# A two-layer conditioned block on one core: first norm spread from its root, stacked condition parts, a new order of the steps

## Chip, core and metric

One of the eight cores of a Trainium2 chip runs the whole kernel. The time is the device time of one execution in microseconds, from the first to the last instruction with what lies around them. TensorE is PE in the profile, VectorE DVE, ScalarE ACT, GpSimd POOL, and SP is the sync engine, which here only issues DMAs.

## What is computed

128 sequences of 64 tokens with 256 features go through a transformer block whose norms are modulated by a condition per sequence, and then through a graph attention with 20 keys. Everything is float32. Cut to what matters:

```python
mods = silu(c) @ adaln_w + adaln_b              # per sequence: shift, scale, gate, twice
x_mod = rms(x) * (1 + scale_msa) + shift_msa    # first norm
q, k, v = split(x_mod @ qkv_w); q, k = rope(rms(q)), rope(rms(k))
x = x + gate_msa * (softmax(q k^T / 4) v @ proj_w + proj_b)
h = rms(x) * (1 + scale_mlp) + shift_mlp        # second norm
x = x + gate_mlp * (silu(h @ w1) * (h @ w3) @ w2)
# graph layer: v = x, q = c
row_zero = v.sum(-1) == 0
self_feat = [v, where(row_zero, 0, q)] @ W_self.T + b_self
for d in range(2):                              # adjacency and its transpose, 20 keys, 11 labels
    aff = where(A.sum(-1) > 0, q1 k1^T / 4, NEG) + A @ w_bias
    out += softmax(aff) @ kv @ Wout[d]
y = v + relu(self_feat + out)
```

## The kernel before

The 128 sequences are cut into 32 blocks of 4 sequences (MB), 256 tokens (MT). Activations lie transposed, features on the partitions in DC = 2 chunks of 128, tokens along the free axis. A float32 matmul of the large weights is made of three products of rounded parts: `w_lo` and `w_hi` with the high part, `w_hi` with the low part of the activation (`high_terms`, `low_terms`, all recorded at L456, the helper `linear`). ScalarE rounds the high part (L831, L878, L893, L905, L916), GpSimd subtracts it for the low part (L1290).

All work of a block is cut into named steps, and for each engine a list in `ORDER` (L79 to L114) says in which order it does them. An entry (a, step, n) does part n of the step for block m + a in iteration m, so several blocks are in flight: on TensorE in iteration m the graph layer of block m, the MLP of block m + 1, the attention of block m + 2 and the first norm's transposition of block m + 3. `run_steps` (L148) writes out the first and last iterations and makes a loop of the others. Engines meet only by semaphores: `wait` waits for this block's producer, `wait_free` for the last reader of a PSUM bank (`BANK`, L71 to L75, says which of the eight 2 KB banks a step writes).

First norm, before. SP loads x by tokens (x_in). ScalarE squares it with a running sum (L811), GpSimd makes the mean's inverse root (L1278, L1280), ScalarE multiplies the token rows by it (L818), TensorE transposes the rows in four pieces (L496), VectorE multiplies by the scale out of PSUM (L1057) and adds the shift (L1076). VectorE first copies the block's conditions to a small tile (L1051, and L1062 for the second norm), by a product with ones.

Second norm, before. ScalarE squares x1 (L824); TensorE sums over features with a column of 1/256, tile by tile and chunk by chunk, four matmuls that the profile shows as eight instructions (L504); VectorE adds epsilon (L1047), GpSimd takes the power -1/2 (L1286), TensorE transposes the broadcast root, which spreads it over all partitions (L511), and VectorE multiplies x1, already scaled by GpSimd (L1312), by it (L1067), then adds the shift.

Self feature, before. TensorE sums the rows (`rowsum`, a product with ones) and multiplies by W_self (L674 to L681). VectorE makes a gate of 128 rows (L1179): row b is one where the token belongs to sequence b and its sum isn't zero. `self_cond` (L683) then adds the condition part with four matmuls, `cond_lo` and `cond_hi` by two output chunks. VectorE adds the bias (L1188).

Other steps that the text names. VectorE: `edge_masks` (L1201 to L1204, its scaling L1202), `score_max` and `score` (L1120, L1125: maximum and subtraction of the attention's scores), `k1` (L1211), `score1_bias`, `score1_max`, `score1` (graph scores), `mix` (L1131, L1134), `mix1` (L1250), `qkv` (L1087 to L1100), `rope_scale` (L1104), `rope` (L1110), `mlp_up` (L1159 to L1168), `mlp_down` (L1173), `edges` (L1195), `out` (L1256). TensorE: `heads` (L540), `score` (L557), `probsT` (L577), `mix` (L592), `mixT` (L601), `v1` (L727), `score1` (L744), `probsT1` (L761), `mix1` (L775). GpSimd: `heads` spreads the keys (L1302), `proj` adds the residual (L1323), `mlp_down` adds x1 (L1327).

At the start SP loads the condition, nine small constants, the first weight pieces and x; ScalarE's queue loads the condition weights. VectorE waits for all constants (L978) before it forms the silu of the condition, TensorE makes the twelve modulations (L476), VectorE adds their biases (L1033). Weight pieces are staged in free tiles (`HOME`) and split by ScalarE and VectorE behind certain steps (`HIGH_PARTS`, `LOW_PARTS`).

## Time and profile before

| | us |
|---|---|
| median of 3 runs | 1485.19 (1482.28 to 1488.89) |
| profiled execution, its own time | 1483.07 |
| its span, first to last instruction | 1481.2 |
| TensorE busy in it | 1345.6 (91%) |
| VectorE busy | 1189.3 (80%) |
| ScalarE busy | 899.2 (61%) |
| GpSimd busy | 657.3 (44%) |

The mean granted TensorE clock is 0.975 of full speed. Times below are from one profiled execution, counted from the start of its span. Matmuls are pipelined and their ends are modelled: in a run of them the next starts before the end of the one before, so the length of a step on TensorE is best read from its start to the start of what follows.

### The profile page before, as it was taken

To read this page: it belongs to the slowest core of one execution; us is meant where nothing else is said; L and a number is where in the kernel's file an instruction comes from. 1 tells how busy PE (TensorE), PEld (TensorE's weight loads), DVE (VectorE), ACT (ScalarE), POOL (GpSimd) and SP (SyncE) were. 2 spreads that over 40 slices of the span, in tenths; PEclk is the share of its full clock that TensorE was granted. 3 is DMA by queue.
4 is the path that set the end of the run, shared out by engine and by line. 5 is a ranking of instruction groups with operands and counts; after the bars stand their busy time and mean duration, and the time that the engine had idled before them with its cause. 6 is when DMAs were issued, how large, how long until landed. Compare 5 with 4: busy or idle time off the path is not lost. (4 is left out here: it accounts for less than half of the span.)

```text
span 1481.2 us, 51674 instructions
## 1 busy us (share of the span) xinstructions
PE 1345.6 (91%) x20532; PEld 1243.1 (84%) x20532; DVE 1189.3 (80%) x2137; ACT 899.2 (61%) x1744; POOL 657.3 (44%) x580
## 2 busy tenths in 40 slices
PE   4589999999999999999999999999999999999985
PEld 3479888888888888988888898888888888888885
DVE  5558888888888888888888888888888888888853
ACT  3456566667666666666666676666667666666632
POOL 0134444544444454444445444444544444454441
PEclk9589999999999999999999999999999999999998
DMA  5200111110011111001111100111110011110000
GB/s 171 65 27 2 36 35 33 33 33 21 12 33 33 33 33 33 17 16 33 33 33 33 33 12 21 33 33 33 33 33 12 21 33 33 33 33 26 3 27 16
DMA packets 40307, 47.28 MB, mean 32 GB/s; under 512 B 3536, under 2 KB 38224, under 8 KB 40272
## 3 DMA queue, kind: packets, MB, share of 16 engines
q1 hardware_dynamic: 39424, 44.94, 10.0%
q10 hardware_dynamic: 848, 1.84, 0.3%
q8 instruction: 26, 0.43, 0.1%
q14 instruction: 9, 0.07, 0.0%
HBM read 38.38 MB, written 8.39 MB: 32 GB/s over the span
## 5 line engine op out<-in xcount | busy, mean ns | idle before, releaser
L456 PE MATMUL psum<-nh,w_lo 128*128 128x256 f32 x704 | 181.8, 293 | 0.7 <-DVE gf L1168 0.6
L1290 POOL TENSOR_TENSOR nl<-xn,nh 128x512 fp32r<-128x512 f32 x64 | 82.8, 1294 | 221.3 <-ACT nh L831 221.3
L456 PE MATMUL psum<-nh,w_hi 128*128 128x256 f32 x704 | 172.7, 280 | 0.9 <-issue 0.9
L1290 POOL TENSOR_TENSOR gl<-gf,gh 128x512 fp32r<-128x512 f32 x96 | 123.6, 1287 | 105.2 <-ACT gh L893 105.2
L456 PEld LDWEIGHTS psum<-nh,w_lo 128*128 128x128 f32 x704 | 133.6, 190 | 7.5 <-issue 7.0
L456 PEld LDWEIGHTS psum<-nh,w_hi 128*128 128x128 f32 x704 | 133.8, 190 | 1.1 <-issue 1.1
L1346 POOL TENSOR_TENSOR e<-e,inv 128x640 f32<-128x640 f32 x64 | 81.5, 1273 | 99.4 <-DVE inv L1245 99.3
L456 PE MATMUL psum<-nl,w_hi 128*128 128x256 f32 x704 | 115.6, 283 | 0.0
L831 ACT ACTIVATE nh<-xn 128x512 fp32r<-128x512 f32 x64 | 40.4, 631 | 106.3 <-DVE xn L1076 106.1
L1302 POOL TENSOR_TENSOR kbd<-qkT,hmask 128x512 f32<-128x512 f32 x64 | 66.5, 1040 | 86.2 <-ACT qkT L859 86.2
L456 PEld LDWEIGHTS psum<-nl,w_hi 128*128 128x128 f32 x704 | 95.3, 189 | 3.4
L864 ACT ACTIVATE e<-e 128x1024 f32<-128x1024 f32 x64 | 68.1, 1064 | 49.6 <-DVE e L1125 49.6
L1087 DVE TENSOR_TENSOR qs<-psum,sinw 128x512 f32<-128x512 f32 x64 | 44.2, 691 | 66.5 <-ACT qk_sq L839 62.2
L1327 POOL TENSOR_TENSOR x<-x 128x512 f32<-128x512 f32 x32 | 41.0, 1282 | 124.1 <-DVE x L1173 124.1
L456 PE MATMUL psum<-qkv_lo,nh 128*128 128x512 f32 (+1 forms) x256 | 86.2, 348 | 4.8 <-ACT nh L831 4.8
L456 PE MATMUL psum<-gh,w_lo 128*128 128x256 f32 x320 | 83.0, 291 | 0.0
L456 PE MATMUL psum<-qkv_hi,nh 128*128 128x512 f32 (+1 forms) x256 | 82.2, 343 | 0.0
L1120 DVE TENSOR_REDUCE mx<-psum 128x16 f32<-128x1024 f32 x64 | 78.1, 1220 | 4.1 <-PE psum L557 0.8
L893 ACT ACTIVATE gh<-gf 128x512 fp32r<-128x512 f32 x96 | 60.7, 632 | 32.4 <-DVE gf L1168 30.3
L456 PE MATMUL psum<-gh,w_hi 128*128 128x256 f32 x320 | 79.5, 280 | 0.0
L592 PE MATMUL psum<-vb,pT 128*64 128x34 f32 x2048 | 73.7, 227 | 6.3 <-ACT pT L873 3.2
L1125 DVE TENSOR_TENSOR e<-psum,mx 128x1024 f32<-128x1024 f32 x64 | 76.5, 1195 | 3.4
(187 smaller groups left out, 4418.2 us busy)
## 6 DMA issues: line engine op xcount, KB each, us to landing
adj<-in_adj SPq DMA_DIRECT2D x32, 440.0 KB, 3.3
x_in<-in_x SPq DMA_DIRECT2D x32, 256.0 KB, 3.0
x_res<-in_xT SPq DMA_DIRECT2D x32, 256.0 KB, 3.2
out_T<-y SPq DMA_DIRECT2D x32, 256.0 KB, 2.2
e<-in_adaln ACTq DMA_DIRECT2D x2, 512.0 KB, 5.5
stage<-in_qkv SPq DMA_DIRECT2D x2, 384.0 KB, 5.6
pT<-in_w SPq DMA_DIRECT2D x2, 384.0 KB, 7.2
stage<-in_w SPq DMA_DIRECT2D x2, 384.0 KB, 6.6
```

Source lines behind the costliest of these rows:

```text
L456: last = nc.tensor.matmul(out, lhsT, rhs, start=start and i == 0, stop=stop and i == len(terms) - 1)
L592: last = nc.tensor.matmul(mix_ps[t][s * S:(s + 1) * S, j, :], pT0[:, j, s * S:(s + 1) * S], vb[:, t, s, j, :], start=True, stop=True, tile ...
L831: nc.scalar.activation(nh[norm][:, :, :], xn[norm][:, :, :], ACT.Copy).then_inc(normed_hi[norm].sem, 1)
L864: nc.scalar.activation(e0[t][:, :, :], e0[t][:, :, :], ACT.Exp, scale=DH ** -0.5).then_inc(exps.sem, 1)
L893: nc.scalar.activation(gh[:, 2 * n:2 * n + 2, :], gf[:, :, :], ACT.Copy).then_inc(g_hi.sem, 1)
L1087: nc.vector.tensor_tensor(qs[:, :, :, :], qk_ps, sinw[:, :, :].unsqueeze(2).to_broadcast([P, 2, H, DH]), ALU.mult).then_inc(sin_part.sem, 1)
L1120: nc.vector.tensor_reduce(mx0_v, s_v[t], AX.X, ALU.max).then_inc(maxima.sem, 1)
L1125: nc.vector.tensor_tensor(e0_v[t], s_v[t], mx0_v.unsqueeze(3).to_broadcast([P, NG, 4, S]), ALU.subtract).then_inc(shifted_s.sem, 1)
L1290: return nc.gpsimd.tensor_tensor(out, full, hi.bitcast(F32), ALU.subtract)
L1302: nc.gpsimd.tensor_tensor(kbd[:, t, :, :, :, :].rearrange("p c s h k -> p (c s) h k"), qkT[t][:, 1, :, :].rearrange("p c (s k) -> p (c s) ...
L1327: nc.gpsimd.tensor_tensor(x2[:, :, :], x2[:, :, :], x1[:, :, :], ALU.add).then_inc(x2_done.sem, 1)
L1346: nc.gpsimd.tensor_tensor(e_v, e_v, inv1[t][:, :].unsqueeze(2).to_broadcast([P, ND * H, NKV]), ALU.mult)\
```

## The change

- **First norm.** SP now also loads the transposed x into `xn[0]` (`load_xT`). GpSimd multiplies it by the scale (`norm0_scale`), TensorE transposes the broadcast root in two pieces (`norm0_apply`), VectorE multiplies by the spread root and adds the shift. The scaling of the token rows on ScalarE and the four transpositions are gone. ScalarE squares in place.
- **Squares summed by chunks.** A VectorE step `norm1_squares` adds the two chunks of the second norm's squares; TensorE sums two tiles in place of four pieces.
- **Stacked condition parts.** High and low part of the condition product are written to DRAM once; SP loads for each block 8 rows (high and low of four sequences). The gate has 8 rows, and `self_cond` has two matmuls in place of four.
- **Self bias** is added by ScalarE in place of VectorE. The copies of the block's conditions are gone: the steps read `mods` itself.
- **At first** VectorE waits for the constants after the condition's silu, ScalarE adds the biases of eight of the twelve modulations, and pieces of the weights are loaded in another order to other homes.
- **All orders and PSUM banks** are new.

The diff, cut to its core (bank waits, declarations and unchanged context left out):

```diff
 BANK = {
-    "xT": 4, "qk": (1, 5), "v": (2, 4), "heads": (0, 2), "probsT": (2, 6, 5, 3), "probsT1": (0, 2, 3, 7),
-    "mix": (6, 3), "q1": (1, 4), "score": 3, "score1": 3, "mixT": 6, "proj": 7, "norm1": 2, "up": (1, 2, 7),
-    "gate": (3, 7, 0), "down": 1, "rowsum": 5, "self": 0, "k1": 6, "v1": 0, "mix1": 2,
+    "xT": 6, "qk": (2, 3), "v": (7, 1), "heads": (7, 5), "probsT": (5, 4, 4, 0), "probsT1": (0, 5, 4, 7),
+    "mix": (5, 6), "q1": (4, 6), "score": 0, "score1": 0, "mixT": 6, "proj": 2, "norm1": 7, "up": (6, 4, 6),
+    "gate": (3, 1, 0), "down": 1, "rowsum": 3, "self": 4, "k1": 5, "v1": 7, "mix1": 5,
 }
 ORDER = {
     "PE": [
...
+        (2, "heads", 1), (1, "proj", 0), (0, "self", 0), (0, "self_cond", 0), (2, "score", 0), (0, "k1", 0),
+        (0, "q1", 0), (1, "norm1_mean", 0), (0, "q1", 1), (1, "norm1_apply", 0), (2, "probsT", 0),
+        (3, "norm0_apply", 0), (0, "score1", 0), (0, "v1", 0), (2, "mix", 0), (2, "probsT", 1), (1, "mlp_up", 0),
+        (1, "mlp_up", 1), (3, "qkv", 0), (0, "probsT1", 0), (2, "mix", 1), (3, "qkv", 1), (0, "mix1", 0),
+        (0, "probsT1", 1), (1, "mlp_up", 2), (0, "mix1", 1), (1, "mlp_down", 0), (1, "mlp_down", 1), (2, "mixT", 0),
+        (3, "heads", 0),
     ],
     "DVE": [
...
+        (2, "rope", 0), (2, "rope", 1), (0, "mlp_down", 0), (1, "mixT", 0), (1, "proj", 0), (0, "row_mask", 0),
+        (0, "edge_masks", 0), (2, "score_max", 0), (2, "score", 0), (1, "norm1_squares", 0), (2, "score_max", 1),
+        (1, "norm1_mean", 0), (0, "k1", 0), (2, "score", 1), (1, "norm1_apply", 0), (1, "norm1_shift", 0),
+        (3, "norm0_apply", 0), (3, "norm0_shift", 0), (0, "score1_bias", 0), (0, "score1_max", 0),
+        (0, "score1_bias", 1), (0, "score1", 0), (2, "mix", 0), (0, "score1_max", 1), (0, "soft1", 0),
+        (0, "soft1_inverse", 0), (1, "mlp_up", 0), (0, "score1", 1), (0, "soft1", 1), (0, "soft1_inverse", 1),
+        (1, "mlp_up", 1), (2, "mix", 1), (3, "qkv", 0), (3, "qkv", 1), (1, "mlp_up", 2), (0, "mix1", 0),
+        (1, "edges", 0), (3, "rope_scale", 0), (0, "out", 0),
     ],
     "Activation": [
...
+        (2, "rope_scale", 0), (0, "mlp_split", 2), (1, "mixT", 0), (2, "heads", 0), (2, "heads", 1),
+        (0, "x2_split", 0), (0, "self", 0), (1, "norm1_mean", 0), (0, "keys", 0), (0, "self_split", 0),
+        (3, "norm0_mean", 0), (2, "score", 0), (0, "q1", 0), (0, "q1", 1), (2, "probsT", 0), (2, "score", 1),
...
     "Pool": [
...
+        (1, "proj", 0), (0, "self_split", 0), (3, "norm0_mean", 0), (1, "norm1_mean", 0), (1, "norm1_scale", 0),
+        (3, "norm0_scale", 0), (1, "norm1_apply", 0), (3, "norm0_apply", 0), (0, "soft1", 0), (1, "mlp_up", 0),
+        (0, "soft1", 1), (1, "edges", 0), (1, "mlp_up", 1), (1, "mlp_up", 2), (1, "mlp_down", 0), (3, "heads", 0),
+        (1, "x2_split", 0), (3, "heads", 1),
     ],
     "SP": [
-        (3, "norm0_mean", 0), (2, "mlp_up", 0), (0, "out", 0), (2, "norm0_apply", 0),
+        (0, "self", 0), (3, "norm0_mean", 0), (1, "mlp_up", 0), (3, "norm0_scale", 0), (2, "norm0_apply", 0),
+        (0, "out", 0),
     ],
...
+            def load_xT(m, n):
+                wait_last(sp, normed_lo[0], m)
+                sp.dma_start(xn[0][:, :, :], x_v[:, :, bass.ds(m * MT, MT)]).then_inc(xT_in_s.sem, 16)
...
+            def load_cond_rows(m, n):
...
+                wait_last(sp, self_ps, m)
+                sp.dma_start(cond_rows[:, :].bitcast(F32), cond_parts[bass.ds(m, 1), :, :, :].rearrange("m i b n -> (m i b) n"))\
+                    .then_inc(cond_rows_s.sem, 16)
...
             def norm0_apply(m, n):
...
                 for t in range(TILES):
-                    for c in range(DC):
-                        last = nc.tensor.transpose(xT_ps[:, c, t * P:(t + 1) * P], x_tok[:, t, c * P:(c + 1) * P], ident[:, :])
-                last.then_inc(xT_done.sem, 1)
+                    last = nc.tensor.transpose(spread0_ps[:, t * P:(t + 1) * P],
+                                               rms_inv[0][:, t:t + 1].to_broadcast([P, P]), ident[:, :])
+                last.then_inc(spread[0].sem, 1)
...
                 for t in range(TILES):
-                    for c in range(DC):
-                        last = nc.tensor.matmul(ms1_ps[:, t:t + 1], x1_sq[:, c, t * P:(t + 1) * P],
-                                                mean_col[:, :], start=c == 0, stop=c == DC - 1)
+                    last = nc.tensor.matmul(ms1_ps[:, t:t + 1], x1_sq[:, 0, t * P:(t + 1) * P], mean_col[:, :],
+                                            start=True, stop=True)
...
             def self_cond(m, n):
                 wait(pe, row_gate, m, 1)
+                wait(pe, cond_rows_s, m, 16)
                 for o in both:
-                    last = linear(self_out[:, o, :], [(w[:, out_chunks[o]], gate[:, :]) for w in (cond_lo, cond_hi)], False, o == DC - 1)
+                    last = linear(self_out[:, o, :], [(cond_rows[:, out_chunks[o]], gate[:, :])], False, o == DC - 1)
...
+            def self_feat(m, n):                    # on ScalarE
+                wait(act, self_ps, m, 1)
+                wait_last(act, relu_done, m)
+                for o in range(DC):
+                    nc.scalar.activation(sf[:, o, :], self_out[:, o, :], ACT.Identity, bias=self_b[:, o:o + 1])\
+                        .then_inc(self_done.sem, 1)
...
+            def norm1_squares(m, n):
+                wait(dve, squares[1], m, 1)
+                nc.vector.tensor_tensor(x1_sq[:, 0, :], x1_sq[:, 0, :], x1_sq[:, 1, :], ALU.add).then_inc(square_sums.sem, 1)
...
-            def self_feat(m, n):
-                wait(dve, self_ps, m, 1)
-                wait_last(dve, relu_done, m)
-                for o in range(DC):
-                    nc.vector.tensor_scalar(sf[:, o, :], self_out[:, o, :], self_b[:, o:o + 1], None, ALU.add)\
-                        .then_inc(self_done.sem, 1)
...
+            def norm0_scale(m, n):                  # on GpSimd
+                wait(pool, xT_in_s, m, 16)
+                nc.gpsimd.tensor_tensor(by_seq(xn[0][:, :, :]), by_seq(xn[0][:, :, :]),
+                                        per_seq(mods[:, SCALE_A:SCALE_A + DC, bass.ds(m * MB, MB)]), ALU.mult)\
+                    .then_inc(scaled[0].sem, 1)
```

## Rows read from the trace of the kernel before

**Rows 1.** Busy time of the engines in one steady interval
```profile
core 0: us, PE busy (x) PEld busy (x) DVE busy (x) ACT busy (x) POOL busy (x), PEclk, DMA share, GB/s
700.00:743.30 43.30, 40.99 (x642) 37.97 (x642) 36.49 (x65) 27.73 (x55) 20.56 (x19) 1.00 0.10 29
```

**Rows 2.** Second root's transposition: ns min/median/max, first and last start us
```profile
L511 PE MATMUL psum<-ident,rms_inv x64: 270/272/474, 83.4 to 1423.8; 128*128 128x128 f32 x64
```

**Rows 3.** Timeline, TensorE, steady interval: start us, us, engine, line, operation
```profile
710.83 1.09 PE L577 MATMUL psum<-ident,e 128*128 128x128 f32 x8
...
712.75 1.13 PE L592 MATMUL psum<-vb,pT 128*64 128x34 f32 x32
...
716.96 0.39 PE L456 MATMUL psum<-aoh,proj_lo 128*128 128x256 f32 x1 [0.69 <-ACT aoh L878]
...
718.49 0.60 PE L496 MATMUL psum<-ident,x_tok 128*128 128x128 f32 x4
...
721.76 0.38 PE L456 MATMUL psum<-gate,cond_lo 128*128 128x256 f32 x1 [0.81 <-DVE gate L1179]
...
722.34 0.42 PE L456 MATMUL psum<-qkv_lo,nh 128*128 128x512 f32 x1
...
724.46 0.40 PE L456 MATMUL psum<-qkv_lo,nh 128*128 128x512 f32 x1
...
728.30 0.99 PE L504 MATMUL psum<-mean_col,x_sq 128*128 128x1 f32 x8
...
733.07 0.66 PE L540 MATMUL psum<-ident,qr 128*128 128x128 f32 x4 [0.71 <-DVE qr L1110]
733.66 1.51 PE L744 MATMUL psum<-kbd,q1T 32*64 32x40 f32 x128
...
735.52 0.36 PE L456 MATMUL psum<-nh,w_lo 128*128 128x256 f32 x1
...
743.55 1.21 PE L557 MATMUL psum<-kbd,qkT 32*64 32x128 f32 x64
```

**Rows 4.** Masks' scaling on VectorE: ns min/median/max, first and last start us
```profile
L1202 DVE TENSOR_SCALAR edge_n<-edge_n x32: 194/1193/1207, 104.0 to 1442.1; 128x80 f32<-128x80 f32 x32
```

**Rows 5.** Timeline, VectorE, the same interval
```profile
702.21 1.22 DVE L1120 TENSOR_REDUCE mx<-psum 128x16 f32<-128x1024 f32 x1
...
707.33 0.41 DVE L1162 SCALAR_TENSOR_TENSOR gf<-th,psum 128x256 f32<-128x256 f32 x1
...
708.30 0.69 DVE L1168 TENSOR_TENSOR gf<-gf,psum 128x512 f32<-128x512 f32 x1
709.62 1.07 DVE L1201 TENSOR_REDUCE edge_v<-q1T 128x80 f32<-128x880 f32 x1 [0.63 <-POOL q1T L1331]
710.60 1.19 DVE L1202 TENSOR_SCALAR edge_n<-edge_n 128x80 f32<-128x80 f32 x1
...
712.05 0.25 DVE L1131 RECIPROCAL inv<-psum 128x16 f32<-128x16 f32 x1
...
712.74 0.88 DVE L1250 SCALAR_TENSOR_TENSOR sf<-psum,bout,sf 128x256 f32<-128x256 f32 x2
...
725.28 0.69 DVE L1087 TENSOR_TENSOR qs<-psum,sinw 128x512 f32<-128x512 f32 x1 [1.87 <-ACT qk_sq L839]
...
730.51 1.25 DVE L1211 SCALAR_TENSOR_TENSOR kbd<-psum,colb,hmask 128x160 f32<-128x160 f32 x4
731.67 0.54 DVE L1104 RECIPROCAL qk_inv<-qk_root 128x64 f32<-128x64 f32 x1
```

**Rows 6.** Timeline, GpSimd, the same interval
```profile
710.46 1.28 POOL L1290 TENSOR_TENSOR gl<-gf,gh 128x512 fp32r<-128x512 f32 x1 [0.88 <-ACT gh L893]
...
736.53 1.03 POOL L1302 TENSOR_TENSOR kbd<-qkT,hmask 128x512 f32<-128x512 f32 x1
```

**Rows 7.** DMA issues: KB each, median us from issue to landing
```profile
x_res<-in_xT SPq DMA_DIRECT2D x32, 256.0 KB, 3.2
...
edge_b<-in_edge_b SPq DMA_DIRECT2D x1, 0.5 KB, 5.5
```

**Rows 8.** Waits: us in total, times, longest
```profile
DVE th L981 <- DMA freq<-in_freq: 5.0, 1, 5.0
```

More of the change, by code:

```diff
@@ L80 @@
     "PE": [
-        (0, "self", 0), (0, "self_cond", 0), (2, "qkv", 0), (2, "qkv", 1), (0, "k1", 0), (1, "norm1_mean", 0),
-        (0, "q1", 0), (0, "q1", 1), (1, "norm1_apply", 0), (2, "heads", 0), (0, "score1", 0), (2, "heads", 1),
-        (1, "mlp_up", 0), (0, "v1", 0), (1, "mlp_up", 1), (2, "score", 0), (0, "probsT1", 0), (1, "mlp_up", 2),
-        (1, "mlp_down", 0), (2, "probsT", 0), (0, "probsT1", 1), (0, "mix1", 0), (2, "mix", 0), (2, "probsT", 1),
-        (0, "mix1", 1), (2, "mix", 1), (1, "mlp_down", 1), (2, "mixT", 0), (2, "proj", 0), (3, "norm0_apply", 0),
+        (2, "heads", 1), (1, "proj", 0), (0, "self", 0), (0, "self_cond", 0), (2, "score", 0), (0, "k1", 0),
@@ L86 @@
+        (0, "q1", 0), (1, "norm1_mean", 0), (0, "q1", 1), (1, "norm1_apply", 0), (2, "probsT", 0),
[3 more added lines that the diff above has]
+        (3, "heads", 0),
     ],
     "DVE": [
-        (1, "mlp_up", 2), (1, "edge_masks", 0), (2, "mix", 0), (0, "mix1", 0), (0, "out", 0), (2, "mix", 1),
@@ L89 @@
-        (1, "mlp_down", 0), (2, "mixT", 0), (2, "edges", 0), (2, "proj", 0), (3, "norm0_scale", 0),
-        (3, "norm0_shift", 0), (1, "row_mask", 0), (1, "self", 0), (3, "qkv", 0), (3, "qkv", 1), (2, "norm1_mean", 0),
[3 rows of a table removed]
-        (2, "mlp_up", 1), (1, "soft1", 1), (3, "score_max", 0), (3, "score", 0), (3, "score_max", 1),
-        (1, "soft1_inverse", 1), (3, "score", 1),
+        (2, "rope", 0), (2, "rope", 1), (0, "mlp_down", 0), (1, "mixT", 0), (1, "proj", 0), (0, "row_mask", 0),
+        (0, "edge_masks", 0), (2, "score_max", 0), (2, "score", 0), (1, "norm1_squares", 0), (2, "score_max", 1),
[4 rows of a table added]
@@ L96 @@
+        (1, "mlp_up", 1), (2, "mix", 1), (3, "qkv", 0), (3, "qkv", 1), (1, "mlp_up", 2), (0, "mix1", 0),
+        (1, "edges", 0), (3, "rope_scale", 0), (0, "out", 0),
     ],
     "Activation": [
-        (2, "qkv", 1), (2, "rope_scale", 0), (0, "q1", 0), (0, "q1", 1), (2, "heads", 0), (1, "norm1_apply", 0),
-        (1, "edges", 0), (1, "mlp_up", 0), (2, "heads", 1), (0, "score1", 0), (1, "mlp_split", 0), (1, "mlp_up", 1),
-        (0, "v1", 0), (0, "score1", 1), (1, "mlp_split", 1), (0, "probsT1", 0), (2, "score", 0), (3, "norm0_mean", 0),
@@ L101 @@
-        (1, "mlp_up", 2), (2, "probsT", 0), (2, "score", 1), (1, "mlp_split", 2), (0, "probsT1", 1), (2, "probsT", 1),
-        (3, "norm0_rows", 0), (2, "mixT", 0), (1, "x2_split", 0), (3, "norm0_apply", 0), (1, "self_split", 0),
-        (3, "qkv", 0), (1, "keys", 0), (2, "norm1_mean", 0),
+        (2, "rope_scale", 0), (0, "mlp_split", 2), (1, "mixT", 0), (2, "heads", 0), (2, "heads", 1),
+        (0, "x2_split", 0), (0, "self", 0), (1, "norm1_mean", 0), (0, "keys", 0), (0, "self_split", 0),
@@ L104 @@
+        (3, "norm0_mean", 0), (2, "score", 0), (0, "q1", 0), (0, "q1", 1), (2, "probsT", 0), (2, "score", 1),
+        (1, "norm1_apply", 0), (0, "v1", 0), (3, "norm0_apply", 0), (1, "edges", 0), (0, "score1", 0),
+        (2, "probsT", 1), (1, "mlp_up", 0), (1, "mlp_split", 0), (0, "score1", 1), (1, "mlp_up", 1),
+        (0, "probsT1", 0), (3, "qkv", 0), (1, "mlp_split", 1), (3, "qkv", 1), (0, "probsT1", 1), (1, "mlp_up", 2),
     ],
     "Pool": [
-        (0, "x2_split", 0), (2, "norm0_apply", 0), (1, "proj", 0), (0, "self_split", 0), (1, "norm1_scale", 0),
@@ L210, in build_program @@
         rms_inv = [sb(f"rms_inv{i}", [P, TILES]) for i in range(2)]
-        mod = [sb(f"mod{i}", [P, NMOD, MB]) for i in range(2)]
         nh = [sb(f"nh{i}", [P, DC, MT], F32R) for i in range(2)]
@@ L248, in build_program @@
         sf = sb("sf", [P, DC, MT])
-        gate = sb("gate", [P, MT], F32R)
+        gate = sb("gate", [2 * MB, MT], F32R)
+        cond_rows = sb("cond_rows", [2 * MB, D], F32R)
         kv = sb("kv", [P, DC, MB, NKP])
@@ L678, in self_feat @@
                 wait(pe, x2_lo, m, 1)
-                linear(rowsum_ps, [(ones_r[:, :], nl[1][:, c, :]) for c in both], start=False).then_inc(rowsum.sem, 1)
+                linear(rowsum_ps, [(ones_r[:, 0:M_SUM], nl[1][:, c, :]) for c in both], start=False).then_inc(rowsum.sem, 1)
                 for o in both:
@@ L1144, in proj @@
             def proj(m, n):
+                if isinstance(m, int) and m == 0:
+                    dve.wait_ge(mods_set_a.sem, NMOD - 4)
                 wait(dve, proj_done, m, 1)
```

284 lines of the change are left out of this document (146 added, 138 removed), and 3 rows, old and new, of the table ORDER.

## The prediction

> **What bounds the kernel now.** I read the busy table by stage first. In one steady stretch of 43.3 us TensorE is busy 41.0, VectorE 36.5, ScalarE 27.7, GpSimd 20.6, and the granted clock is full [rows 1]. One block of four sequences takes that long: the transposition of the second norm's root runs from 83.4 to 1423.8 over 32 blocks, 31 intervals of 43.24 us [rows 2]. So three parts make the span: 83.4 us of filling, 31 intervals, and 57.4 us (1481.2 less 1423.8) of draining. Then the timeline of TensorE in one interval. It stands still only three times: 0.69 us before the projection (ScalarE's rounding of the mixed heads), 0.81 before the condition step (VectorE's row gate), 0.71 before the first heads transposition (VectorE's rotated heads) [rows 3]. So in the steady part TensorE is the bound, with 2.2 us of waits, and an edit pays if it takes TensorE's work or one of these waits away, until VectorE, 6.8 us behind, is reached.
>
> **What the parts do to each engine, per block.**
> *TensorE.* The condition step goes from four matmuls to two; the four take 0.58 us (721.76 to 722.34) [rows 3], so 0.3 goes. A matmul with 8 rows in place of 128 has no row of its own; I take it as long as a full one, and even at nothing it would give only 0.3 more. The four transpositions of normed rows (0.60, of which 0.27, the length of a single one [rows 2], is the tail of the last) become two of a root: 0.2 less. The means go from eight instructions (0.99 with tail) to four: 0.4 less [rows 3]. The projection's wait of 0.69 goes, since both heads transpositions now stand between mixT and proj (0.6 each); the gate's wait shrinks from 0.8 to about 0.2, since VectorE's first-norm steps no longer stand ahead of the gate. TensorE alone, with the heads' wait gone too, could do 43.3 - 0.3 - 0.2 - 0.4 - 0.7 - 0.6 - 0.7 = 40.4 us.
> *VectorE.* Two copies of the conditions go (48 elements, 0.2 each, as the quickest of the masks' scalings of 80 [rows 4]) and the self bias (two of 0.44, as mix1's two of the same size) goes to ScalarE; the sum of squares by chunks comes, 256 elements, which costs about 0.4 as half the 0.69 of 512 [rows 5]. The first norm's multiplication stays. Net 0.9 less: 35.6 busy. *ScalarE* loses two scalings of x and gains two biases of the same width: nothing, and it idles a third of the time [rows 1]. Its table loads stay two a block. *GpSimd* gains the first norm's scale, 1.05 us as its other products of this form (kbd 1.03) [rows 6], laid between two waits; if its cover went, the MLP's low part would come 1.05 later, and TensorE has mix and a transposition before it. *DMA.* A second transposed x (256 KB) and an 8 KB condition load a block, 0.1 of the DMA time now being used [rows 1]; the x load lands in some 3.2 us [rows 7] and is issued, behind the edge masks' wait, some 6 us before its use. SP's queue is in order: the condition load (waits for the self feature of the block before, long done), x, edges (wait for the masks, at 7.8 on the clock below), transposed x, residual x (waits for GpSimd's addition, at 6.8), the store (waits for out, the last step). Behind the masks' wait only loads stand that have over 5 us to their use, so I cost the queue at nothing but for the condition rows, a rival below.
>
> **The new order, followed round once.** The sum of work doesn't say what the order gives, so I place the steps on a clock that starts when VectorE begins mlp_down(0), its third step.
> 1. VectorE 0.69 for its 512 elements; GpSimd in its new order adds (1.28, as all its products of 512 plain elements), spreads keys (1.03, now between) and takes the low part of x2 (1.28): with four handoffs of 0.05 it is 4.5 us [rows 5, 6].
> 2. TensorE's last row sums, the gate (256 elements, 0.41 as the MLP's row of that size), handoffs: 0.9. At 5.4.
> 3. VectorE: edge masks 2.43 (709.62 to 712.05); both maxima and both subtractions 4.87 (702.21 to 707.33 less a reciprocal's 0.25); sum of squares 0.4; k1 1.25: 9.0 us with the small ones [rows 5]. At 14.4.
> 4. TensorE could be at score1(0) at about 13.9, but that shares a PSUM bank with score(2) and waits for VectorE's second subtraction. Then score1 1.45, mix and transposition 1.06 and 1.02, both MLP stages with v1 8.03 (735.52 to 743.55), qkv 2.12 (722.34 to 724.46), transposition 1.02, mix 1.06: 15.7, each row less the 0.07 by which it overlaps the next, with handoffs 15.8 [rows 3]. At 30.2.
> 5. VectorE: mix 0.69, two qkv steps 5.16 (725.28 to 730.51, less 0.07), third MLP stage 1.66, mix1 0.88, edges 1.07 (the reduction of 880 elements), rope_scale 0.65 (0.54 and a handoff), out and two ropes of 0.69, less the 0.08 by which operations in a row overlap: 11.9 us [rows 5]. At 42.1, where mlp_down of the next block begins. Its matmuls were done 0.8 us before.
> So the interval is **42.1 us**, VectorE's chain and no more TensorE alone: 1.7 us above TensorE's bound, 1.2 below 43.3. One term has two values in the trace: the masks' scaling of 80 elements takes 1193 ns as a rule but 194 at its quickest [rows 4]; in the steady interval it starts 0.14 us after a GpSimd operation and ends as that ends [rows 5, 6]. In the new order GpSimd's addition of the residual lies there for only some 0.4, so 0.6 could be won back; I keep it as reserve for steps that now meet GpSimd and didn't before.
>
> **A rule beside it.** In the trace the pair just named shows VectorE held for about 1.0 us, while VectorE's additions of two SBUF operands fall where GpSimd idles [rows 4, 6]. The Trainium skill (SBUF — State Buffer, Who interferes with whom) says that also a VectorE instruction with two SBUF inputs and a GpSimd one that reads SBUF exclude each other for a whole instruction. The trace agrees for the scaling alone. What that could do is the second rival.
>
> **Filling and draining.** VectorE waits 5.0 us at the start for the last small constant before it makes the conditions [rows 8]; the new code waits after. At best all 5.0 is won. Against it, qkv(1) now stands ahead of proj(0): two of 2.12, twice that at half clock, up to 8.5 us. Between -5 and +8.5 I take +1: the first root at 84. Block 0 to 1 lacks the graph steps, the last interval the qkv steps (5.2 of VectorE): 37 us each. The last block's chain is the same: 57.4.
> Sum: 84 + 37 + 29 x 42.1 + 37 + 57.4 = 1436.3 us span; the profiled execution had 1.9 outside its span (1483.1 against 1481.2), so 1438 against its 1483. The median of the runs, 1485.2, is 2.1 higher: **1440 against the median**.
>
> **Rivals.**
> *TensorE stays the bound (0.12).* VectorE's steps overlap their neighbours a little more than I summed, the masks' 0.6 comes free, and score1's wait disappears: 40.4 us. Speaks for it: VectorE would be busy 35.6 of 40.4. Against: the waits before self, the means, the root and score1 would all have to go at once. 29 x 1.7 less: 1391.
> *GpSimd holds VectorE (0.16).* In my round norm0_shift starts within 0.1 us of GpSimd's low part, the squares' sum meets its roots, the additions of qkv meet gl. Each held step in a chain piece costs about 1.0 (1193 less 194) [rows 4]. One such step: 43.1, 1440 + 29 = 1469 (0.08). From the second on, 2.0 against the 1.2 gained, the change loses: **1498 with two, 1527 with three (0.08 together)**. Against it: norm0_shift has 1.4 us of slack before TensorE's second mix, and no two-operand addition of the trace was ever held. By the rule of the Trainium skill's SBUF page all three could be held.
> *The condition rows come late (0.07).* SP issues their load after the store, 0.5 us before my clock's zero, and the condition step wants them at 5.4. A load lands in 3.2 us as a rule, the smallest took 5.5 at the start [rows 7]: on time both ways. At 7.2 us each block would lose 1.3: 1440 + 38 = 1478. So this is the case in which the new form brings nothing.
> *The fill is mis-sized*: -6 to +8 on any case.
>
> **Chances.** My own round 0.65 (1420 to 1460, the interval 41.5 to 42.7). About 0.5%, 7.4 us, is what a measurement of this kernel can tell from no change, so faster means below 1478: 0.65 + 0.12 + 0.08 and nothing of the late rows, 0.85. Slower 0.08, the two or more held steps; same 0.07. The range leaves out most of the first rival and the losing case: 1400 to 1472.
>
> **What would show it.** Interval between the second norm's transpositions near 42.1; no wait of TensorE before proj, about 0.2 before the condition step, 0.5 before score1 on VectorE's subtraction and 0.5 before self on ScalarE's rounding; VectorE at 85%. Wrong would be: an interval at 40.4 with VectorE waiting before mlp_down; a two-operand VectorE step of 1.5 us; TensorE waiting for a DMA before the condition step; a first root far from 84.

## The result, and the profile after

The changed kernel takes 1421.39 us in the median of four runs (1416.22 to 1426.24), the kernel before 1485.87 on the same chip: a ratio of 0.9566, with a 95% interval of 0.9521 to 0.9612. The profiled execution has a span of 1416.1 us and a mean granted clock of 0.977. Its page's busy times:
```profile
PE 1342.2 (95%) x20276; PEld 1229.1 (87%) x20276; DVE 1135.2 (80%) x2033; ACT 878.6 (62%) x1752; POOL 712.1 (50%) x612
```

The changed kernel's transposition of the second norm's root, one pair a block (first and last start; against [rows 2]):
```profile
L541 PE MATMUL psum<-ident,rms_inv x64: 272/272/476, 79.1 to 1358.3; 128*128 128x128 f32 x64
```
and its busy time in one steady interval (against [rows 1]; columns: PE, PEld, DVE, ACT, POOL, granted clock, DMA share, GB/s):
```profile
700.00:741.40 41.40, 41.13 (x635) 37.68 (x634) 34.78 (x63) 26.97 (x55) 22.33 (x19) 1.00 0.12 36
```
Filling takes 79.1 us instead of 83.4, draining 57.8 (1416.1 less 1358.3) instead of 57.4, and the 31 intervals sum to 1279.2 instead of 1340.4. So 61 of the 65 us came from the intervals. In the steady part each is 41.41 us (43.29 before). "Interval" below is always the median distance of these transpositions in the trace.

TensorE now shows busy for 99% of an interval, and its recorded waits over 28 intervals are gone. Waits of TensorE in the changed kernel, 160 to 1340 us (us in total, times, longest):
```profile
PE psum L775 <- issue: 1.0, 2, 0.7
```
The timeline of VectorE in one steady interval (start, us, engine, line, operation; idle before it and what ended that), cut to the rows used, against [rows 5]:
```profile
718.43 0.26 DVE L1162 RECIPROCAL inv<-psum 128x16 f32<-128x16 f32 x1 [1.36 <-PE psum L622]
...
720.85 1.36 DVE L1130 TENSOR_TENSOR qr<-qc,qs 128x256 f32<-128x256 f32 x2
...
724.04 0.75 DVE L1130 TENSOR_TENSOR qr<-qc,qs 128x256 f32<-128x256 f32 x2
...
727.06 1.06 DVE L1221 TENSOR_REDUCE edge_n<-adj 128x80 f32<-128x880 int32 x1
...
729.04 1.28 DVE L1141 TENSOR_TENSOR qr<-qr,qk_inv 128x512 f32<-128x512 f32 x2
730.24 0.68 DVE L1206 TENSOR_TENSOR x<-psum,mods 128x512 f32<-128x512 f32 x1
731.33 0.69 DVE L1171 TENSOR_TENSOR aol<-psum,aoh 128x512 fp32r<-128x512 f32 x1 [0.40 <-ACT aoh L911]
733.28 0.88 DVE L1182 SCALAR_TENSOR_TENSOR x<-psum,colb,mods 128x256 f32<-128x256 f32 x2 [1.26 <-PE psum L486]
735.13 0.41 DVE L1212 SCALAR_TENSOR_TENSOR gate<-psum,hot 8x256 fp32r<-8x256 f32 x1 [0.97 <-PE psum L486]
735.47 1.05 DVE L1227 TENSOR_REDUCE edge_v<-q1T 128x80 f32<-128x880 f32 x1
736.44 0.38 DVE L1228 TENSOR_SCALAR edge_n<-edge_n 128x80 f32<-128x80 f32 x1
```
Two things are to be seen. From the second mix (718.43) to mlp_down (730.24) VectorE has no idle time at all, and before and after that it waits for TensorE (1.36, 1.26, 0.97). This is the round of the prediction in its outline: TensorE's stretch, then VectorE's, then short steps by turns. Who closes the stretch between the condition step and score1 is another question; it is answered below. And the first pair of L1130 takes 1.36 us, the second 0.75: the first runs beside a GpSimd instruction. GpSimd in the same interval, against [rows 6]:
```profile
720.30 1.29 POOL L1315 TENSOR_TENSOR gl<-gf,gh 128x512 fp32r<-128x512 f32 x1 [1.36 <-ACT gh L926]
727.26 1.29 POOL L1315 TENSOR_TENSOR gl<-gf,gh 128x512 fp32r<-128x512 f32 x1 [5.67 <-ACT gh L926]
731.00 1.29 POOL L1360 TENSOR_TENSOR x<-x 128x512 f32<-128x512 f32 x1 [2.45 <-DVE x L1206]
```
On my clock (mlp_down at 730.24 is 0) the condition step's matmuls stand at 5.44:
```profile
735.68 0.49 PE L486 MATMUL psum<-gate,cond_rows 8*128 8x256 f32 x2
```
VectorE's second subtraction of the attention's scores, and TensorE's score1 behind it:
```profile
742.65 1.21 DVE L1156 TENSOR_TENSOR e<-psum,mx 128x1024 f32<-128x1024 f32 x1
```
```profile
744.26 1.50 PE L775 MATMUL psum<-kbd,q1T 32*64 32x40 f32 x128
```
The subtraction is done at 743.86, and score1 starts 0.40 later; the prediction had score1 wait for it. Over the steady blocks the two stand at 13.6 and 14.0 on the clock (medians).

### The profile page after: what moved, and what is told of

Its sections match the earlier page's. It is cut to its first block, busy times and chain, and to the rows that moved or that the text cites. A ratio compares the mean times of both kernels' runs of the same rounds, so it can differ in the third digit from the quotient of the medians.

```text
span 1416.1 us, 51305 instructions
## 1 busy us (share of the span) xinstructions
PE 1342.2 (95%) x20276; PEld 1229.1 (87%) x20276; DVE 1135.2 (80%) x2033; ACT 878.6 (62%) x1752; POOL 712.1 (50%) x612
## 4 chain that ended last, share of the span: by engine, by line
PE 73%; issue 9%; POOL 7%; ACT 3%; DVE 1%; ACTq 0%; POOLq 0%; DVEq 0%
PE psum L486 39%; PE psum L607 5%; PE psum L622 5%; PE psum L728 4%; PE psum L792 4%; PE psum L758 4%; PE psum L775 3%; POOL nl L1315 3%; PE psum L587 3%; PE psum L806 2%; POOL gl L1315 2%; POOL kbd L1327 2%; ACT gh L926 1%; PE psum L534 1%; ACT qkT L892 1%
## 5 line engine op out<-in xcount | busy, mean ns | idle before, releaser
L486 PE MATMUL psum<-nh,w_hi 128*128 128x256 f32 x704 | 176.8, 282 | 0.0
L1315 POOL TENSOR_TENSOR nl<-xn,nh 128x512 fp32r<-128x512 f32 x64 | 99.2, 1551 | 127.3 <-ACT nh L864 127.3
L946 ACT ACTIVATE sf<-psum,colb 128x256 f32<-128x256 f32 x64 | 26.8, 470 | 103.3 <-PE psum L486 103.3
L1151 DVE TENSOR_REDUCE mx<-psum 128x16 f32<-128x1024 f32 x64 | 78.1, 1221 | 14.4 <-PE psum L587 14.1
L911 ACT ACTIVATE aoh<-psum 128x512 fp32r<-128x512 f32 x32 | 19.1, 598 | 109.2 <-PE psum L631 109.2
L607 PE MATMUL psum<-ident,e 128*128 128x128 f32 x512 | 77.9, 289 | 4.3 <-ACT e L897 4.2
L622 PEld LDWEIGHTS psum<-vb,pT 128*64 128x64 f32 x2048 | 66.6, 140 | 12.8 <-issue 12.5
```

What stands on the lines that cost most here:

```text
L486: last = nc.tensor.matmul(out, lhsT, rhs, start=start and i == 0, stop=stop and i == len(terms) - 1)
L607: last = nc.tensor.transpose(pT_out[t][j // 4][:, j % 4, :], e0[t][:, 2 * pair(j):2 * pair(j) + 2, :].rearrange("p h s -> p (h s)"), ident ...
L622: last = nc.tensor.matmul(mix_ps[t][s * S:(s + 1) * S, j, :], pT0[:, j, s * S:(s + 1) * S], vb[:, t, s, j, :], start=True, stop=True, tile ...
L1151: nc.vector.tensor_reduce(mx0_v, s_v[t], AX.X, ALU.max).then_inc(maxima.sem, 1)
L1315: return nc.gpsimd.tensor_tensor(out, full, hi.bitcast(F32), ALU.subtract)
```

## The experiments

The theory was that the interval is a round through both engines: TensorE from score1 to the second mix (piece 4), VectorE from there to mlp_down (piece 5), and a chain of short steps between mlp_down and score1 (pieces 1 to 3). The rival was that TensorE's work alone is the bound, as 99% busy suggests. All ratios are against the kernel before on the same chip.

**Six matmuls fewer, at two places.** These two runs tell the theories apart. Both leave out six of the MLP's matmuls, those with the low part of the weight (so that part of x·w is not computed), one run in the second stage, one in the third:
```
-  linear(out[:, c, :], high_terms(w, out_chunks[j], nh[1], both), c == 0, False)
+  terms = high_terms(w, out_chunks[j], nh[1], both)
+  linear(out[:, c, :], terms[1::2] if n == 1 and (name, c) != ("w3", 1) else terms, c == 0, False)
   (the other run: if n == 2)
```


> In the second MLP stage six of its 24 matmuls are left out (the low part of the weight for three of four output chunks), some 0.75 us of TensorE's time, in the stretch between score1 and the second mix where VectorE waits for TensorE. Both theories (TensorE's work alone is the bound; TensorE and VectorE take turns in one round) expect the interval 0.7 shorter, 40.7, and some 1400 us.

> In the third MLP stage six of its 18 matmuls are left out, the same 0.75 us of TensorE's time, but beside the stretch in which my round runs through VectorE (second mix to mlp_down). TensorE's work alone as the bound: interval 40.7 and 1400 us, as in the run above. The round by turns: VectorE begins mlp_down 0.3 us after TensorE's last matmul for it, so the interval stays at 41.3 to 41.4, 1417 to 1421 us.

Measured: in piece 4 1403.04 us (1401.88 to 1407.19), ratio 0.9467 (0.944 to 0.9495), interval 40.67, 0.74 shorter. In piece 5 1424.63 us (1420.51 to 1426.06), 0.9596 (0.9569 to 0.9624), interval 41.42, no shorter. The same work is worth its full time at one place and nothing at the other. The second root's transposition, the run in piece 4 and then the run in piece 5:
```profile
L541 PE MATMUL psum<-ident,rms_inv x64: 272/272/473, 78.2 to 1338.5; 128*128 128x128 f32 x64
```
```profile
L541 PE MATMUL psum<-ident,rms_inv x64: 270/272/473, 79.2 to 1363.9; 128*128 128x128 f32 x64
```
Of the run in piece 5 also TensorE's waits and the busy windows, 160 to 1340 us:
```profile
PE psum L486 <- POOL gl L1316: 8.1, 28, 0.3
```
```profile
160.00:1340.00 1180.00, 1158.33 (x17851) 1052.14 (x17850) 988.02 (x1762) 765.94 (x1530) 632.47 (x538) 1.00 0.11 36
```
In the run in piece 5, TensorE's third MLP stage is 0.67 us shorter, from its start to the start of what follows, but mlp_down behind it is 0.48 longer and the projection 0.16. Only 0.3 of that is recorded as a wait, for GpSimd's low part of the gated values, which itself waits for VectorE's and ScalarE's steps of the third stage; the rest stands in a busy time that contains standing still (it falls from 1170.64, shown below, to 1158.33, by 0.43 an interval). TensorE's work alone is not the bound, although it shows 99% busy. The rival fell.

**Self bias back on VectorE.** In the new order, right behind the row gate:
```
 DVE: (1, "proj", 0), (0, "row_mask", 0), + (0, "self", 0), (0, "edge_masks", 0), ...
 ACT: (0, "x2_split", 0), - (0, "self", 0), (1, "norm1_mean", 0), ...
```


> The changed kernel with the self bias back on VectorE, between the gate and the edge masks. Loop theory: VectorE waits for self there and takes 0.9, so score_max starts about 1.2 us later and TensorE's score1, which has only some 0.2 us to spare, waits; interval up by 0.8 to 1.1, span about 1445. Rival (VectorE has slack, TensorE's work is the bound): within 0.2 us of 41.4, span 1416 to 1422.

Measured: 1451.65 us, ratio 0.9802 (0.9775 to 0.983), interval 42.27, 0.86 longer. TensorE's matmuls didn't change at all. The cost is VectorE's, as the round says, but TensorE meets it before the means of the second norm and not before score1, where it was expected (160 to 1340 us):
```profile
PE psum L534 <- DVE x_sq L1085: 12.9, 28, 0.5
```
That 0.86 is near the two biases' own 0.88 is in part chance: the masks start 1.5 later, as VectorE also waits for the self feature's matmuls (0.66), and 0.6 of it is won back, since VectorE no longer waits for the scores (0.39) and the masks' scaling isn't held (0.19).

**The other three parts, undone one by one in the new order.** First norm by token rows (two scalings of x on ScalarE, four transpositions on TensorE):
```
- transpose(spread0_ps[:, t * P:(t + 1) * P], rms_inv[0][:, t:t + 1].to_broadcast([P, P]), ident)
+ for c in range(DC): transpose(xT_ps[:, c, t * P:(t + 1) * P], x_tok[:, t, c * P:(c + 1) * P], ident)
+ ACT norm0_rows: activation(x_tok[:, t, :], x_in[:, t, :], ACT.Identity, scale=rms_inv[0][:, t:t + 1])
```


> The changed kernel with the first norm by token rows as before: two scalings on ScalarE between its q1 steps, four transpositions in place of two, no scale on GpSimd, no second load of transposed x. TensorE's work theory: 0.1 to 0.2 more per block, span 1419 to 1422. Loop theory: ScalarE's 0.9 falls where it has 0.56 to spare, 0.3 later for the probabilities' copies, interval 41.4 to 41.7, span 1416 to 1425. If the spread root were the main gain of the change: over 1440.

Measured 1426.13, ratio 0.9613 (0.9586 to 0.9639), interval 41.57. Squares not summed by chunks:
```
- nc.tensor.matmul(ms1_ps[:, t:t + 1], x1_sq[:, 0, t * P:(t + 1) * P], mean_col[:, :], start=True, stop=True)
+ for c in range(DC): nc.tensor.matmul(ms1_ps[:, t:t + 1], x1_sq[:, c, ...], mean_col[:, :], start=c == 0, ...)
```


> The changed kernel (interval 41.40 us) with TensorE summing all four pieces of squares again and no sum by chunks on VectorE. TensorE's own work sets the interval: 0.4 more, 41.8, span about 1429. The round through VectorE sets it: VectorE's stretch from edge masks to the second subtraction is 0.37 shorter, nothing or a little less, 41.2 to 41.4, span 1410 to 1416.

Measured 1432.46, ratio 0.9656 (0.9624 to 0.9689), interval 41.66. This is a miss of the round as I had it: with VectorE closing the stretch up to score1, less work for VectorE should have cost nothing (41.2 to 41.4). TensorE's four more instructions set the time there; it is nearer to the other case's 41.8. Condition step as before, 128 rows, four matmuls, no load:
```
- linear(self_out[:, o, :], [(cond_rows[:, out_chunks[o]], gate[:, :])], ...)
+ linear(self_out[:, o, :], [(w[:, out_chunks[o]], gate[:, :]) for w in (cond_lo, cond_hi)], ...)
```


> The changed kernel with the 128-row gate, four condition matmuls and no load of condition rows. They stand in the round itself (gate, condition step, score) and in TensorE's work, so both theories say 0.2 more: 41.6, span about 1423. If the load of the rows were felt in the changed kernel, this would be no slower or faster, 41.4 or less.

Measured 1428.37, ratio 0.9641 (0.9606 to 0.9676), interval 41.60. The intervals grow by 0.16, 0.25 and 0.19. The copies of the block's conditions stay away in every run here, so what their removal is worth was not measured. The medians of the first and third lie within their runs' scatter of the changed kernel's, so the interval of the trace is the better witness there.

**All parts, old order.** Every new operation, with the order and the PSUM banks of before; the chunk sum stands between the two qkv steps on VectorE:
```
 DVE: (3, "norm0_shift", 0), (1, "row_mask", 0), (3, "qkv", 0), + (2, "norm1_squares", 0), (3, "qkv", 1), ...
 ACT: (1, "x2_split", 0), (3, "norm0_apply", 0), + (1, "self", 0), (1, "self_split", 0), ...
 SP:  (3, "norm0_mean", 0), + (3, "norm0_scale", 0), (2, "mlp_up", 0), + (1, "self", 0), (0, "out", 0), ...
```


> All the new operations (spread root, sum of squares by chunks, 8 condition rows, bias on ScalarE, new start) in the old order with the old banks. If the parts bring what their instructions cost on TensorE (0.3 + 0.1 + 0.5) and the waits before proj (0.7) and before the condition step (0.8) stay: interval 43.3 - 0.9 = 42.4, span about 1453. If the order were worth nothing: 41.4 and about 1416 to 1425. If the parts are worth nothing by themselves: 43.3 and about 1478.

Measured: 1482.1 (1480.25 to 1484.62), ratio 1.0005 (0.9992 to 1.0017), interval 43.47: nothing was gained. A miss of 1.1 us an interval. The waits of TensorE there, 160 to 1340 us:
```profile
PE psum L568 <- DVE qr L1139: 29.0, 27, 1.1
PE psum L484 <- ACT aoh L909: 18.5, 27, 0.7
PE psum L484 <- DVE gate L1210: 16.9, 27, 0.6
```
Before, the same three stood at 0.71, 0.69 and 0.81 [rows 3]. TensorE had some 0.9 less to do. The gate's wait fell by 0.2, the wait for the rotated heads, which VectorE finishes in one unbroken stretch from the first qkv step, grew by 0.4. The rest of the saving is lost in steps that show busy; the next run says more on where.

**The same without the chunk sum.** The sum is VectorE's in that stretch, so it was suspected:
```
-  (3, "qkv", 0), (2, "norm1_squares", 0), (3, "qkv", 1), ...    and the means over both chunks on TensorE
+  (3, "qkv", 0), (3, "qkv", 1), ...
```


> The parts in the old order, but the squares of the second norm not summed by chunks on VectorE. If that sum, placed between the two steps of qkv, was what held the rotated heads and ate the parts' gain, TensorE's wait before the first heads transposition falls from 1.1 to 0.7, the interval from 43.47 to 43.1, 1470 us. If the old order's round is closed elsewhere, 43.4 to 43.5 and 1480.

```profile
PE psum L484 <- ACT aoh L910: 18.5, 27, 0.7
PE psum L484 <- DVE gate L1211: 16.3, 27, 0.6
PE psum L569 <- DVE qr L1140: 15.9, 28, 0.6
```
Measured: interval 43.34, 1477.38 us (1476.19 to 1481.53), ratio 0.9966 (0.9945 to 0.9986). The wait fell as the first theory said, from 1.1 to 0.6, the interval by 0.13 only: TensorE had the means' 0.4 more to do in exactly that place. So the sum is worth nearly nothing either way there, and the old order's round is closed elsewhere. From mixT to qkv it is 6.39 us in the parts' run against 6.72 before, a real gain of 0.33; from the first qkv matmul to the first heads transposition 10.92 against 10.73; and over the rest 26.16 against 25.84, lost within TensorE's MLP stages without a recorded wait (8.5 us for the three against 8.2). What stretches them is no single wait: the 256-column matmuls on the normed x start 114 ns apart (median) in the kernel before, and 119 to 120 in the changed kernel and all runs made from it, in either order, at a granted clock of 1.00 in both. Over 66 matmuls a block that is 0.3 us. The weights' new homes are common to all these runs, but so is the rest of the new start; why the matmuls follow each other more slowly was not tested.

**The new order alone.** The edits of the four single runs together, with the order, the banks and the start of the changed kernel (these were never separated from one another):
```
 DVE: (1, "proj", 0), (0, "row_mask", 0), + (0, "self", 0), (0, "edge_masks", 0), ... - (1, "norm1_squares", 0)
 ACT: - (0, "self", 0) ... (0, "q1", 0), + (3, "norm0_rows", 0), (0, "q1", 1)
 SP:  - (0, "self", 0), - (3, "norm0_scale", 0)
```


> The new order, banks and start with all four parts undone (token-row norm, four pieces of squares, four condition matmuls, self bias on VectorE). The parts gave nothing in the old order (43.47 against 43.30). If the order is the whole gain, this stays near 41.4 to 41.9 and a span of 1416 to 1435. If the parts are what the new order stands on, their losses add: 41.40 + 0.87 (bias) + 0.17 (norm) + 0.2 (matmuls) + 0 to 0.4 (squares) = 42.7 to 43.0, span 1458 to 1470.

Measured: 1477.45 (1476.2 to 1479.24), ratio 0.9965 (0.995 to 0.9979), interval 43.42. The four single losses sum to 1.46 (0.86, 0.16, 0.25, 0.19), which would be 42.87; it is 2.01. VectorE's timeline tells more than the sum:
```profile
719.78 0.42 DVE L1232 SCALAR_TENSOR_TENSOR gate<-psum,ident 128x256 fp32r<-128x256 f32 x1 [1.10 <-PE psum L492]
721.03 0.88 DVE L1243 TENSOR_SCALAR sf<-psum,colb 128x256 f32<-128x256 f32 x2 [0.83 <-PE psum L492]
721.83 1.06 DVE L1256 TENSOR_REDUCE edge_v<-q1T 128x80 f32<-128x880 f32 x1
722.80 0.19 DVE L1257 TENSOR_SCALAR edge_n<-edge_n 128x80 f32<-128x80 f32 x1
723.03 1.30 DVE L1259 SCALAR_TENSOR_TENSOR edge_bias<-edge_v,edge_b,edge_n 128x80 f32<-128x80 f32 x1
```
and GpSimd beside it:
```profile
722.96 1.27 POOL L1344 TENSOR_TENSOR nl<-sf,nh 128x512 fp32r<-128x512 f32 x1 [1.64 <-ACT nh L971]
```
The addition of the masks (L1259, two operands of 80 in SBUF) takes 1.30 us and ends with GpSimd's instruction, which began 0.07 us before it. With the self bias alone on VectorE (the run above) the same addition began 0.13 before GpSimd's and took 0.30:
```profile
709.89 0.30 DVE L1239 SCALAR_TENSOR_TENSOR edge_bias<-edge_v,edge_b,edge_n 128x80 f32<-128x80 f32 x1
```
```profile
710.02 1.31 POOL L1324 TENSOR_TENSOR nl<-sf,nh 128x512 fp32r<-128x512 f32 x1 [1.57 <-ACT nh L958]
```
So 0.2 us of phase decides over 1.0 us of VectorE, and the hold (1.0) is more than the 0.55 that the four single losses leave unexplained. The clock shows how the rest cancels. Here the masks start at 7.05 instead of 5.24. From there VectorE wins 0.19 at the scaling, 0.39 at the scores that it no longer waits for and 0.33 for the sum by chunks, and loses the 1.0: 1.9 later at its second subtraction by this sum, 2.01 measured, and the whole 2.01 is there when score1 starts (16.03 instead of 14.02). TensorE waits for VectorE in that stretch (160 to 1340 us):
```profile
PE psum L548 <- POOL rms_inv L1340: 30.1, 28, 1.1
```
The root comes from VectorE's addition to the means. So VectorE closes the stretch here, and what the means and the condition step cost TensorE ahead of that wait falls into it. Parts or order alone give 0.0 to 0.4%, both together 4.3%.

**GpSimd's low part of x2 first.** The two key spreads stand around that step on GpSimd; here it comes ahead of both:
```
-  (1, "mlp_down", 0), (3, "heads", 0), (1, "x2_split", 0), (3, "heads", 1),
+  (1, "mlp_down", 0), (1, "x2_split", 0), (3, "heads", 0), (3, "heads", 1),
```


> The changed kernel with one swap in GpSimd's list: the low part of x2 before the first key spread instead of behind it. The changed kernel's interval is 41.38 us. Loop theory (VectorE's tail, GpSimd's add, key spread and low part, then self on TensorE close the round, and TensorE only looks full): the low part comes 1.0 us earlier, TensorE's stalls inside self (about 0.3) and before the last row sums (0.1) go, the interval falls to about 41.0 and the span from 1416 to about 1404. Rival (TensorE's own work sets the interval): nothing, 1416. The second key spread ends at the same time either way, so no loss is expected from score.

Measured: 1445.81 (1444.8 to 1453.62), ratio 0.976 (0.9741 to 0.9779), interval 42.06, 0.65 longer, where a gain was expected. GpSimd and TensorE in that run:
```profile
705.99 1.30 POOL L1360 TENSOR_TENSOR x<-x 128x512 f32<-128x512 f32 x1 [2.44 <-DVE x L1206]
708.03 1.30 POOL L1315 TENSOR_TENSOR nl<-x,nh 128x512 fp32r<-128x512 f32 x1 [0.74 <-ACT nh L938]
709.28 2.04 POOL L1327 TENSOR_TENSOR kbd<-qkT,hmask 128x512 f32<-128x512 f32 x2
```
```profile
PE psum L587 <- POOL kbd L1327: 24.8, 27, 0.9
```
The low part has to wait for ScalarE's rounding of the sum, 0.74 us in which GpSimd now stands idle; the key spread had filled that gap. TensorE gets the low part earlier and then waits 0.9 for the spread keys before its scores. I had priced the moved step by its own length and not asked what its predecessor was.

**Edge count moved into VectorE's idle time.** The reduction of 1.06 us at the end of piece 5 goes between mixT and proj, where VectorE waits 1.26 us:
```
-  (1, "edges", 0), (3, "rope_scale", 0), (0, "out", 0),
+  (3, "rope_scale", 0), (0, "out", 0),       and (0, "edges", 0) behind (1, "mixT", 0)
```


> The changed kernel with the edge count (1.06 us of VectorE) taken from the tail, where VectorE is busy from the second mix to mlp_down, and put between mixT and proj of the next iteration, where VectorE idles 1.26 us. Loop theory: ropes and mlp_down come earlier, mlp_down by the 0.25 that it starts after its matmuls, and the interval falls by 0.2 to 0.3 to about 41.15, span about 1408. If TensorE's work is already the bound: 41.4, 1416.

Measured: 1422.53 (1421.83 to 1423.17), ratio 0.9592 (0.9565 to 0.9619), interval 41.39: no change. First reading: VectorE is not in the round. The trace doesn't bear that out. VectorE and GpSimd in that run, and the output's line in all 32 blocks (ns min/median/max):
```profile
729.07 1.60 DVE L1282 SCALAR_TENSOR_TENSOR y<-sf,x 128x512 f32<-128x512 f32 x1
730.60 1.28 DVE L1141 TENSOR_TENSOR qr<-qr,qk_inv 128x512 f32<-128x512 f32 x2
```
```profile
728.83 1.30 POOL L1315 TENSOR_TENSOR gl<-gf,gh 128x512 fp32r<-128x512 f32 x1 [5.69 <-ACT gh L926]
```
```profile
L1282 DVE SCALAR_TENSOR_TENSOR y<-sf,x x32: 692/1578/1766, 148.8 to 1416.9; 128x512 f32<-128x512 f32 x32
```
The output's addition (two SBUF operands) took 1.58 us as a rule instead of 0.63: it now falls beside GpSimd's gl, which the reduction had covered. VectorE's piece 5 lost 1.06 and got 0.95 back. Even without that, not more than 0.3 could have come: in the changed kernel TensorE's last matmul for mlp_down ends at about 730.0, and VectorE begins at 730.24.

**The constants' wait ahead of the silu again**, for the fill:
```
+ dve.wait_ge(consts_in.sem, 16 * len(small))
  dve.wait_ge(cond_tanh.sem, 1)
```


> Changed kernel with VectorE waiting for the last small constant before it makes the conditions, as the kernel before does. If that wait was what the fill won, the first root comes 3 to 5 us later (82 to 84) and the time is 1424 to 1426; if the first loads of x are the limit instead, no change (1421).

Measured: 1423.19 (1420.44 to 1425.0), ratio 0.959 (0.9567 to 0.9612), first root at 79.5 instead of 79.1. TensorE's first wait in that run, and in the changed kernel:
```profile
PE psum L506 <- DVE gf L1025: 11.8, 1, 11.8
```
```profile
PE psum L506 <- DMA x<-in_self_cond: 10.2, 1, 10.2
```
The wait for the constants only took the place of one for a transfer, that of the self feature's condition weights. Taking it away brings the first root 0.4 us earlier.

## Why the prediction was right

It was 1440 us within 1400 to 1472; 1421 came. The mechanism held in its outline: a round in which TensorE's stretch and VectorE's follow each other. One piece of it was closed by the other engine than I had said, and three terms were off.

- *The round.* Predicted 42.1, measured 41.41. Point by point on the same clock: condition step at 5.4 (5.44 measured); VectorE's second subtraction done at 14.4 (13.6); second mix at 30.2 (29.57, which is 718.43 and one interval less 730.24); piece 5 11.9 (11.81).
- *The term that was furthest off in the round is the masks' scaling.* I kept it at 1193 ns and held 0.6 in reserve. It takes 377 (ns min/median/max), and that 0.8 is the difference at 14.4:
```profile
L1228 DVE TENSOR_SCALAR edge_n<-edge_n x32: 179/377/389, 111.1 to 1387.8; 128x80 f32<-128x80 f32 x32
```
  Over 29 intervals the 0.7 by which the interval came out shorter makes 20 us, as much as the whole sum was too high. GpSimd's addition of the residual ends at 736.76 and holds the scaling for only 0.2. I had seen this and counted the safe value instead of the one that my own clock gave.
- *Piece 3 is TensorE's, not VectorE's.* Of the 0.8 only 0.4 reached the interval. The prediction had TensorE ready for score1 at 13.9 and waiting for the subtraction until 14.4. With the subtraction done at 13.6, TensorE's own steps from the condition step on set score1, at 14.0, and the wait that I had there is gone. The run without the sum by chunks agrees (less for VectorE, more for TensorE, 0.25 longer). VectorE is close behind: with the self bias it closes this piece. The other 0.3 of the 0.7: 0.2 from score1 to the second mix (15.6 against 15.8), 0.1 in piece 5.
- *The rival of TensorE alone (1391)* did not happen, and the two runs with six matmuls fewer show why: its work in piece 5 has slack. From the condition step to the second mix, though, it describes what the trace shows. But the opening sentence of the prediction, that in the kernel before TensorE is the bound and an edit pays if it takes TensorE's work away, was wrong: all parts without the order took some 1 us of work and gave nothing. Waits of 2.2 us in all were a sign of a round, not the rest of a bound.
- *The rival of a held VectorE (1469 and more)* came in part: one addition of qkv meets gl and takes 1.03 us instead of 0.42. It cost 0.6 instead of 1.0, as it begins in the middle of GpSimd's instruction, and it was paid from what VectorE's steps overlap more than I summed (piece 5 without it would be 11.2). The order alone and the moved edge count show the full 1.0.
- *Condition rows late (1478):* no wait for them in the trace. *No wait before proj:* right. *Waits before the condition step, score1 and self:* the list of waits has none, but the rows show gaps of 0.1 before the low part of self and before the condition step, with more standing still hidden in the matmul ahead of each (below).
- *VectorE at 85%:* 34.78 of 41.40 is 84%.
- *Fill:* 84 predicted, 79.1 measured. The part that failed is the -5 for the constants, which are worth 0.4. With all parts and the new start in the old order the first root is at 73.8 against 83.4, so these are worth 9.6 us of fill together, which I had not priced; the new order costs 5.3 of them, the direction and over half of the 8.5 given to it. Which of the parts or loads wins the 9.6 was not tested.
- *Short intervals:* 37 each predicted, 37.9 and 36.1 measured, 74.1 together. The 4.2 us that are missing stand in the second and third interval, which I counted as steady: 45.2 and 42.1 instead of 41.41. In the second the mean granted clock is 0.96 and TensorE stands still once for 2.2 us, with no recorded cause. *Drain:* 57.4, 57.8 measured.
- The sum: 4.9 less fill, 20.0 less in the intervals, 4.3 more in the intervals that are not like the steady ones, 0.4 more drain: 1436.3 becomes 1416.1.

The parts pay through the round they stand in: self bias off VectorE 0.86, sum by chunks 0.25, condition rows 0.19, first norm 0.16 an interval, and only with the new order and its banks, in which VectorE's first-norm steps no longer stand before the gate and TensorE has work between mixT and proj. That these two moves are what makes the new order work is argued from the traces; no run moved them alone, and order and banks were only changed together.

## What to carry to other kernels

Follow one round through all engines before pricing an edit: 0.7 us off an engine that is busy 99% was worth all of itself in one stretch and nothing in another. After moving a step, look at what it meets: which idle gap it filled, and which two-operand VectorE step now falls beside GpSimd. Test a part both alone and by taking it out of the finished change, since parts and order each gave next to nothing alone and 4.3% together.
